# Sharing the score banks: PSUM fills of an attention stage rotate over four banks instead of two

## What is computed

```python
gi = concat([q, k, v], -1)                    # q = layernorm(x); k = v = ctx
ig, fg = gi @ igate_w.T + igate_b, gi @ fgate_w.T + fgate_b
cs = cumsum(log_sigmoid(fg))
log_D = where(tril, cs[s] - cs[t], -inf) + ig[t]
D = exp(log_D - max_t log_D)
C = (q k^T / sqrt(dh)) * D
n = maximum(abs(C.sum(-1)), exp(-max_t log_D))
h = C / (n + 1e-6) @ v                        # then a layernorm by head, times out_w
x = x + tanh(g_xattn) * h
...
x = x + tanh(g_ffn) * experts(layernorm(x))   # 8 experts, each on its top-k tokens
```

## Time and profile before

| | us |
|---|---|
| median of 3 runs | 3233.12 (3230.33 to 3277.22) |
| the profiled execution | 3233.75 |
| its span | 3232.0 |
| PE, DVE, ACT, POOL busy | 3043.8, 1850.2, 1136.7, 1055.9 |
| attention ends, about | 1146 |

### The profile page before, as it was taken

One profiled execution on the slowest core, in us unless ns is written; L12 is line 12 of the kernel. 1 busy time (PEld: TensorE's weight loads), 2 busy tenths in 40 slices (PEclk: granted clock), 3 DMA queues, 4 the chain that ended last, 5 costly groups with the idle time before them and its releaser, 6 DMA issues.

```text
span 3232.0 us, 60466 instructions
## 1 busy us (share of the span) xinstructions
PE 3043.8 (94%) x24708; PEld 2407.3 (74%) x24708; DVE 1850.2 (57%) x5188; ACT 1136.7 (35%) x1961; POOL 1055.9 (33%) x1028
## 2 busy tenths in 40 slices
PE   6898998999999939999999999999999999999998
PEld 4777777777777727777777777777778777778786
DVE  5788888888888775435445444444444444453322
ACT  4577676676676632112112111112112112111211
POOL 4566566566566541112111111111111111112111
PEclk8899999999999969999999999999999999999999
DMA  3233433334334143123124213214223223122221
GB/s 110 93 106 119 145 119 119 133 119 137 115 119 146 67 124 77 29 38 95 29 49 92 46 29 82 50 30 104 36 48 75 35 39 103 40 37 62 46 35 22
DMA packets 140060, 250.67 MB, mean 78 GB/s; under 512 B 31456, under 2 KB 31456, under 8 KB 139784
## 3 DMA queue, kind: packets, MB, share of 16 engines
q1 hardware_dynamic: 105784, 170.80, 15.7%
q0 software_dynamic: 28672, 67.65, 12.0%
q10 hardware_dynamic: 5328, 8.36, 0.8%
HBM read 137.23 MB, written 101.19 MB: 74 GB/s over the span
## 4 chain that ended last, share of the span: by engine, by line
PE 60%; DMA 2%; DVE 1%; issue 0%; ACT 0%; POOL 0%; ACTq 0%; DVEq 0%; POOLq 0%
PE DN L1685 30%; PE UP L1659 28%; PE TT L1632 2%; DMA w_raw<-in_L_ffn_W_down 2%; DVE c_hit L1355 0%; DVE down_lo L1221 0%; PE c_bank L1348 0%; ACT z L1604 0%; PE c_bank L1332 0%; DVE c_hit L1376 0%; DVE c_within L1371 0%; ACT down_hi L1215 0%; POOL out_x L1579 0%; DVE mid_lo L1717 0%; DVE c_gained L1408 0%
## 5 line engine op out<-in xcount | busy, mean ns | idle before, releaser
L1579 POOL DMA_INDIRECT out_x<-y,slots x128 | 201.9, 1578 | 1645.0 <-DVE y L1739 1645.0
L1685 PE MATMUL DN<-down_hi,mid_hi 128*128 128x512 f32 x1408 | 579.2, 411 | 0.0
L1659 PE MATMUL UP<-xT_hi,up_hi 128*128 128x512 f32 (+1 forms) x1408 | 553.9, 393 | 4.4 <-ACT z L1604 2.8
L1659 PE MATMUL UP<-xT_hi,up_lo 128*128 128x512 f32 (+1 forms) x1408 | 555.4, 394 | 0.0
L1659 PE MATMUL UP<-xT_lo,up_hi 128*128 128x512 f32 (+1 forms) x1408 | 551.9, 392 | 0.0
L1604 ACT ACTIVATE z<-UP,bup 128x512 f32<-128x512 f32 (+1 forms) x352 | 240.7, 686 | 854.1 <-PE UP L1659 838.7
L1685 PE MATMUL DN<-down_hi,mid_lo 128*128 128x512 f32 x1280 | 505.1, 395 | 0.0
L1685 PE MATMUL DN<-down_lo,mid_hi 128*128 128x512 f32 x1280 | 504.9, 394 | 0.0
L1715 DVE CAST mid_hi<-z 128x512 fp32r<-128x512 f32 (+1 forms) x352 | 151.0, 429 | 484.5 <-ACT z L1604 484.4
L1588 ACT ACTIVATE xT_hi<-TT 128x512 fp32r<-128x512 f32 x126 | 75.0, 596 | 704.2 <-PE TT L1632 683.0
L1659 PEld LDWEIGHTS UP<-xT_hi,up_hi 128*128 128x128 f32 (+1 forms) x1408 | 260.3, 185 | 71.8 <-ACT z L1604 7.4
(11 more groups left out here) (245 smaller groups left out, 5029.2 us busy)
## 6 DMA issues: line engine op xcount, KB each, us to landing
xs<-in_x SPq DMA_DIRECT2D x32, 1024.0 KB, 7.7
kraw<-in_ctx SPq DMA_DIRECT2D x32, 1024.0 KB, 6.6
out_x<-xs SPq DMA_DIRECT2D x32, 1024.0 KB, 5.3
rows_scratch<-xfb SPq DMA_DIRECT2D x32, 1024.0 KB, 4.4
w_raw<-in_L_ffn_W_down SPq DMA_DIRECT2D x40, 512.0 KB, 4.2
w_raw<-in_L_ffn_W_up SPq DMA_DIRECT2D x16, 682.5 KB, 4.1
mid_hi<-mid_hi ACTq DMA_DIRECT2D x32, 86.0 KB
mid_lo<-mid_hi ACTq DMA_DIRECT2D x32, 84.0 KB
```

Of the source, the lines that this page charges most:

```text
L1579: pool.indirect_dma_start(out_rows, bass.IndirectOffsetOnAxis(ap=slots[:, m:m + 1], axis=0), y[:, t, :], None, compute_op=ALU.add).then_in ...
L1659: mm = pe.matmul(UP[k % 3][0:r, :], weights.up[wa][:, c, f * P:f * P + r], xT[xa][:, c, :], start=first, stop=(c == CH - 1 and wa == 1))
L1685: mm = pe.matmul(DN[m % 2][:, :], lhs, rhs, start=first, stop=(f == FCH - 1 and lhs is parts[-1][0]))
```

## The change

Five edits, all in `attention`:

1. **Four banks.** `iteration_fills` now spreads the fills over four banks: 0 and 1 are `T0` and `T1`, 2 and 3 the two banks of `QK`. A bank of `QK` may be filled once the scores in it have been weighed (PE waits for `cc`; the dictionary `weighted`), and scores may be written once the fills in both banks are taken (`cleared`). The special order of i = 1 is gone.
2. **DVE.** `gate_peaks` stands right behind `weighted_queries(b2, 3)`; `head_sums` goes from ahead of it to behind `turned_gates`, and `square_sums(b2, 0)` to between `inner_factors` and `turned_gates`. At the start of an iteration the first `weighted_scores` stands ahead of the first `weighted_queries`.
3. **ACT.** `gate_factors` stands ahead of the first two rows of `first_norm`.
4. **PE.** `product(b3, 3)` stands ahead of `widths(b2, 0)`; `chunk_ends` ahead of `scores(b2, 3)`; `scores(b1, 0)` and `turn_gates` ahead of `turn_rows(b4, 2)`.
5. **POOL.** `weigh_v` stands between the second and the third `add_rows`.

```diff
-            plan = [("qw", b2, 0, "dve", 1), ("q", b1, 0, "act", 0), ("st", b2, 0, "dve", 1), ("k", b1, 0, "act", 0), ("st", b2, 1, "dve", 1),
...
+            plan = [("qw", b2, 0, "dve", 0), ("q", b1, 0, "act", 1), ("st", b2, 0, "dve", 2), ("k", b1, 0, "act", 3), ("st", b2, 1, "dve", 0),
...
+        banks = [T[0], T[1], QK[:, 0, :], QK[:, 1, :]]
...
+            pair = 0
             for kind, b, k, who, side in iteration_fills(i):
+                if kind == "scores":
+                    cleared[b, k] = [latest[n] for n in (2, 3) if n in latest]
+                    pair = k
+                    continue
+                if side >= 2 and i >= 2:
+                    weighted[kind, b, k] = (s["cc"], 2 * (PAIRS * (i - 2) + pair) + side - 1)
...
-                bank[kind, b, k] = T[side]
+                bank[kind, b, k] = banks[side]
...
             if ahead[kind, b, k]:
                 pe.wait_ge(*ahead[kind, b, k])
+            if (kind, b, k) in weighted:
+                pe.wait_ge(*weighted[kind, b, k])
...
                         for j in range(TILES):
+                            if j == 2 and live(b1):
+                                weigh_v(b1)
                             ins = add_rows(pool, b3, j)
...
+                    if live(b1):
+                        gate_factors(b1)
                     if live(i):
                         first_norm(i, (0, 1))
-                    if live(b1):
-                        gate_factors(b1)
...
                     if g:
                         pe.wait_ge(s["cc"], 2 * g)
+                    for taken in cleared.get((b, p), ()):
+                        pe.wait_ge(*taken)
```

More of the change, by code:

```diff
@@ L161, in iteration_fills @@
             b1, b2, b4, b5 = i - 1, i - 2, i - 4, i - 5
-            plan = [("qw", b2, 0, "dve", 1), ("q", b1, 0, "act", 0), ("st", b2, 0, "dve", 1), ("k", b1, 0, "act", 0), ("st", b2, 1, "dve", 1),
[L163 to L171, removed]
+            plan = [("qw", b2, 0, "dve", 0), ("q", b1, 0, "act", 1), ("st", b2, 0, "dve", 2), ("k", b1, 0, "act", 3), ("st", b2, 1, "dve", 0),
+                    ("q", b1, 1, "act", 1), ("st", b2, 2, "dve", 2), ("k", b1, 1, "act", 3),
+                    ("qw", b2, 1, "dve", 0), ("scores", b2, 1, None, None),
+                    ("q", b1, 2, "act", 1), ("k", b1, 2, "act", 2), ("q", b1, 3, "act", 3), ("lg", b5, 0, "act", 0),
+                    ("k", b1, 3, "act", 1),
+                    ("qw", b2, 2, "dve", 0), ("scores", b2, 2, None, None), ("lt", b5, 0, "dve", 0), ("shift", b1, 0, "dve", 0), ("qw", b2, 3, "dve", 0),
+                    ("gates", b1, 0, "dve", 1), ("xfT", b4, 0, "act", 0),
+                    ("xfT", b4, 1, "act", 0), ("turn", b1, 0, "dve", 1), ("xfT", b4, 2, "act", 0), ("xfT", b4, 3, "act", 1)]
             if i == NB + 2:
@@ L178, in iteration_fills @@
             return [f for f in plan if live(f[1])]
-        number, bank, freed, ahead, counts, latest = {}, {}, {}, {}, {"act": 0, "dve": 0}, {}
+        banks = [T[0], T[1], QK[:, 0, :], QK[:, 1, :]]
+        number, bank, freed, ahead, counts, latest, weighted, cleared = {}, {}, {}, {}, {"act": 0, "dve": 0}, {}, {}, {}
         for i in range(NB + 5):
+            pair = 0
             for kind, b, k, who, side in iteration_fills(i):
+                if kind == "scores":
[4 more added lines that the diff above has]
+                    weighted[kind, b, k] = (s["cc"], 2 * (PAIRS * (i - 2) + pair) + side - 1)
                 counts[who] += 1
                 number[kind, b, k] = len(number)
-                bank[kind, b, k] = T[side]
+                bank[kind, b, k] = banks[side]
                 freed[kind, b, k] = (s["ta" if who == "act" else "td"], counts[who])
@@ L399, in _ @@
                         pool.wait_ge(s["x2"], b3 + 1)
-                    if live(b1):
+                    elif live(b1):
                         weigh_v(b1)
@@ L775, in _ @@
                     b1, b2, b3, b4, b5 = i - 1, i - 2, i - 3, i - 4, i - 5
+                    if live(b3):
+                        product(b3, 3)
                     if live(b2):
                         widths(b2, 0)
-                    if live(b3):
-                        product(b3, 3)
                     if live(b1):
@@ L829, in _ @@
                         widths(b2, 3)
+                    if live(b1):
+                        chunk_ends(b1)
+                    if live(b2):
                         scores(b2, 3)
@@ L832, in _ @@
                         turn_rows(b4, 0)
-                    if live(b1):
-                        chunk_ends(b1)
                     if live(b2):
@@ L846, in _ @@
                     if live(b4):
+                        turn_rows(b4, 2)
                         turn_rows(b4, 3)
@@ L1102, in _ @@
                         weighted_queries(b2, 3)
-                    if live(i):
-                        head_sums(i)
-                    if live(b2):
-                        square_sums(b2, 0)
                     if live(b1):
@@ L1112, in _ @@
                         inner_factors(b1)
+                    if live(b2):
+                        square_sums(b2, 0)
+                    if live(b1):
                         turned_gates(b1)
+                    if live(i):
+                        head_sums(i)
                     if live(b2):
```

6 lines of the change are left out of this document (1 added, 5 removed).

## The result

The changed kernel takes 3137.4 us (median of four runs, 3135.8 to 3141.6), against 3255.2 for the kernel before in the same rounds: ratio 0.964, interval 0.955 to 0.974. The kernel before takes about 3230 us in most of its runs and about 3278 us, at a lower granted clock of TensorE, in the others (two of the four here; three runs among the experiments, of 3419, 3910 and 4211 us, had lower ones still and change no median by more than 0.5). Timed again beside its usual runs alone, the changed kernel has 3136.7 against 3229.3, ratio 0.971 (0.970 to 0.973), that is 93 us less. Forecast were 3158.5 in a range of 3142 to 3198.

The account below looks back on a forecast made before the run. A ring of hand-overs, not one engine, was taken to set the 34.13 us period; 28 x 2.48 = 69.4 plus 6 for the edges gave 75 us off 3233.75, so 3158.5, in a range of 3142 to 3198.

Parts of the forecast that it names:

- the wait for `peaks`: PE's wait for DVE's gate_peaks, 1.04 us an iteration from start to start, would go, with peaks ready at 26.7.
- the 0.91: PE's wait of 0.91 us for a turned row's bank, copied by ACT, would go.
- `uv` in time: POOL's uv, two additions ahead of it, would be ready at 34.1 before PE wants it at 34.5: 0.44 us gone.
- a new wait for the first half of the weighed scores: PE's chunk state, now in a bank of QK, would wait for DVE's weighed scores and lose 0.55 us.
- 0.15 for the last turned row: On PE, the last turned row wants the turned gates' bank: about 0.15 us of new wait.
- the walk: The new order timed with the old trace's durations: 2.65 us less an iteration, a period of about 31.5 us.
- The load ring: x2, store and load of xs, DVE statistics, POOL additions with uv: 31.5 us; as binding rival 32.5, 3184, chance 0.24.
- the play between the rings: Late loads of xs above 0.4 us go into PE: 0.15 us added, giving a period of 31.65.
- the slower rival: xs and kraw loads share DMA engines, xs landing in 12.0 instead of 8.8: 16 us more, 3250; chance 0.04.
- The count: Whole kernel: 28 x 2.48 = 69.4 us for iterations 4 to 31, plus 6 for the five edge iterations: 75 us.
- the five edge iterations: Iterations 1 to 3 (lower clock, PE has less to wait) and 32, 33 have part of the chain: 6 us together.
- The lock between DVE and POOL: Two-input DVE operation beside POOL's uv: put at nothing; by a lock DVE stands up to 1.06 us, period 32.5.

Follow-up runs that it names:

- the gates' chain alone: Kernel before, two banks and POOL as before, with gate_peaks, gate_factors, chunk_ends, scores and turned gates pulled forward on DVE, ACT and PE: 3220.1 us, ratio 0.997.
- `uv` last: Changed kernel with weigh_v back behind all four additions on POOL: 3223.7 us, ratio 0.998 to the kernel before.
- load-first kernel: Changed kernel with the next load of xs issued on SP ahead of the store that waits for x2: 3134.5 us, then 3135.6 against 3136.7 for the changed kernel.

## Why the prediction was wrong, point by point

- **The full iterations were right.** Forecast 2.48 us each, measured 2.51; 69.4 us forecast, 70.2 measured. By the steps: the wait for `peaks` gone (right), the 0.91 gone (right), `uv` in time (right), a new wait for the first half of the weighed scores (0.55 forecast, 0.86 in the row), 0.15 for the last turned row (0.19). Two small errors cancel in the agreement to 0.1 us: the short periods are 31.3, where the walk had 31.45 to 31.5, and the mean lies 0.3 above them, where 0.15 was added.
- **The load ring is there, as walked.** It was put at 31.5, with 0.15 us for the play between the rings. The changed kernel waits for the load in 13 of some 22 iterations, and taking the wait out shortens the mean by 0.1 to 0.2, which is within what single executions differ. `xs` lands in 7.4 to 9.1 us (median 8.3, before 7.6) with `kraw` 1 us behind it, far from the 11.4 that the slower rival needs, so that one falls.
- **The failed step is "The count".** The prediction gave the five edge iterations 6 us together, with the reason "lower clock, so PE has less to wait". The rows show the opposite: PE waits more there, 1.85 us for `peaks` against 0.88 in a full iteration, and the clock of 0.82 is itself time to be won. Up to `peaks` of iteration 4 the change saved 18.5 us (143.3 to 144.4 in three executions before, 124.8 in two after), 14.5 of them in iterations 2 and 3, and of those some 11 by the clock and some 4 by waits. The prediction had no term for a clock that rises. For the rest, in iteration 1 and ahead of it, the cause stays open.
- **The end** gave 9.3. Of that, 4.9 us lie ahead of the selection of tokens, in iteration 33 and the drain (in the mean of three executions before and two after it is 3.9), and 4.4 in the later stages, which the change doesn't touch. Those took 2068.3 us in the execution that was the forecast's base, and 2063.8 in two others of the same kernel, against 2063.9 and 2065.3 after. So the 4.4 are no effect of the change: the base itself was some 4 us high, and that much of the 20 was chance.
- **The range was too narrow** at its lower end for the same reason: nearly all of its width was given to the period, and at most 3 us to the edges.
- **What no step had.** The parts are not a sum. In the full iterations the four banks alone and the gates' chain alone gave nothing (34.13 against 34.09 in the mean), the change without POOL's edit lost 0.5 us, and all together gave 2.5; the 8, 11 and 7 us by which these three kernels are faster lie in the iterations at the start and the end. Two things make that. The waits lie on rings, and while one ring holds, the others' gains are lost: at full clock the chain without POOL has 33.6, the banks without the chain 33.3. And in 15 of 28 periods with the banks alone, in 10 with the chain alone and in all without POOL's edit the clock falls for a time, which takes back what was won. The forecasts from waits alone for the banks (22 us, 8 measured) and for `uv` last (33.0, and 34.6 measured: 45 us over 28 periods) fell for that reason. Only for `uv` last is it shown what brings the clock down.
- **The lock between DVE and POOL** was put at nothing, from one row, and that reading was wrong, though it cost little. These are the durations of that operation, L906 in the earlier trace rows with 0.19 us, in the changed kernel (min/median/max) and, one line further, in the load-first kernel:

```profile
L918 DVE TENSOR_TENSOR sm_all<-ex,sx x25: 191/336/357, 228.2 to 986.8; 128x32 f32<-128x32 f32 x25
```

```profile
L919 DVE TENSOR_TENSOR sm_all<-ex,sx x25: 191/323/1217, 225.1 to 982.0; 128x32 f32<-128x32 f32 x25
```

One of the long ones of the load-first kernel, with what POOL does there (two additions, 1.17 us each):

```profile
697.74 2.32 POOL L248 TENSOR_TENSOR xs<-xs,nsb 128x512 f32<-128x512 f32 x2
```

```profile
697.75 1.22 DVE L919 TENSOR_TENSOR sm_all<-ex,sx 128x32 f32<-128x32 f32 x1
```

DVE began 0.01 us behind an addition and ended 0.05 us behind its end. In the changed kernel it begins 0.27 to 0.31 us ahead of the end of a `uv` instruction, and again ends 0.05 us behind it. All 215 of these operations that took over 0.2 us, in ten of the profiled executions, ended 0.045 to 0.053 us behind the end of the POOL instruction that was running when they began. In the row of the kernel before, which merges three instructions of `uv`, the running one ended 0.13 us later: 0.13 + 0.05 is the 0.19 that the operation takes anyway, so that row could not show a wait. This agrees with the Trainium skill, page "SBUF — State Buffer", section "SBUF: two separate sides": whoever starts first keeps the pair of ports for the whole instruction, and the other blocks. What the forecast of 32.5 by that rule had wrong is the size: DVE stands only for what is left of POOL's instruction, here 0.14 us over its 0.19 and not 1.0, and for a whole one in 3 of 25 iterations of one execution, with periods 0.9 to 2.2 us over the usual 31.3.

## What to carry to other kernels

Walk the new order with the durations of the old trace, and close every ring, those over a queue of DMAs too: it gave the period here to 0.1 us. Give the edges of a pipeline the same working, since its waits and TensorE's granted clock differ there. And a wait of TensorE can cost more than its length: look at the granted clock of the stretch, period by period, before judging an edit by its time. Where a short operation of one engine meets a long one of another, look at where in the long one it begins, not only at whether they overlap.

## What the runs showed of the hardware

- Behind one idle stretch of 2.69 us in each iteration TensorE's granted clock stood at 0.50 for about 3 us, so 1.2 instead of 2.4 GHz, at a cost of 1.5 us an iteration; with copies that filled 1.8 us of it the clock was 1.00 from 200 to 1040 us, and the kernel 38 us faster for more work. Shorter waits are not always harmless: behind 0.88 and 0.91 us the clock stayed at 1.00 in 83 of the 84 full iterations of three executions of the kernel before, and fell in 15 of 28 with the four banks alone; with waits of about 1.65 (the chain alone) it fell in 10 of 28.
- A load of 1 MB behind a store, with another load 1 us behind it on the same queue, took 7.4 to 9.1 us from issue to landing (median 8.3), against 7.3 to 8.9 (median 7.6) with the next load 4 us behind the earlier trace rows. Without the store ahead it took 5.6 to 6.9 (median 6.0).
- A DVE operation with two operands in SBUF (0.19 us by itself) that began while POOL's `uv` or an addition to `xs` ran ended 0.045 to 0.053 us behind that POOL instruction, in all 215 cases of over 0.2 us. So it took 0.33 mostly in the changed kernel, around 0.7 in those with `uv` last, and 1.2 in single iterations of the load-first kernel, by where in POOL's instruction it began.
